# Cross-attention: values become the stationary operand, softmax sums come from products with ones, and the combined heads are made without transposes

## The reference

```python
q = split_heads(x, 16); k = split_heads(ctx, 16); v = split_heads(ctx, 16)   # head size 32
logits = einsum('bhqd,bhkd->bhqk', q, k) + bias                              # 154 keys
weights = softmax(logits * (1.0 / sqrt(32)), axis=-1)
attn = einsum('bhqk,bhkd->bhqd', weights, v)
combined = attn.transpose(0, 2, 1, 3).reshape(B, Sq, 512)
x = layernorm(x + combined @ w_out)
```

## Time and profile before

| | |
|---|---|
| median of 3 runs | 2323.93 us (2323.35 to 2326.02) |
| profiled execution | 2313.03 us, span 2311.2 us |
| mean granted PE clock | 0.954 of full speed |
| PE busy | 2112.9 us, 91% |
| DVE busy | 1764.8 us, 76% |
| ACT busy | 1080.5 us, 47% |
| POOL busy | 839.9 us, 36% |
| cross-attention, first to last value matmul | 586 to 1287 us |

### The profile page before, as it was taken

One profiled execution on the slowest core, in us unless ns is written; L12 is line 12 of the kernel. 1 busy time (PEld: TensorE's weight loads), 2 busy tenths in 40 slices (PEclk: granted clock), 3 DMA queues, 4 the chain that ended last, 5 costly groups with the idle time before them and its releaser, 6 DMA issues. The chain is left out here.

```text
span 2311.2 us, 33151 instructions
## 1 busy us (share of the span) xinstructions
PE 2112.9 (91%) x11904; PEld 1150.9 (50%) x11904; DVE 1764.8 (76%) x3345; ACT 1080.5 (47%) x1522; POOL 839.9 (36%) x819
## 2 busy tenths in 40 slices
PE   7999999984999999999999558899999689999998
PEld 3444444431776776777777323344444234444443
DVE  6768686855787998899998465966666388888885
ACT  1444444442554554555555133344444365555551
POOL 2112221322154555456555532222222134444442
PEclk9999999996798999999999879999999899999999
DMA  6334342457789879869963268888888466666662
GB/s 230 107 137 140 103 154 92 128 124 187 202 186 220 212 175 208 233 166 236 243 164 108 70 216 275 235 267 273 268 273 274 198 211 224 235 223 227 232 224 81
DMA packets 386947, 448.53 MB, mean 194 GB/s; under 512 B 279462, under 2 KB 279750, under 8 KB 368352
## 3 DMA queue, kind: packets, MB, share of 16 engines
q1 hardware_dynamic: 322736, 286.14, 44.0%
q0 software_dynamic: 64048, 160.28, 22.3%
HBM read 259.00 MB, written 138.73 MB: 172 GB/s over the span
## 5 line engine op out<-in xcount | busy, mean ns | idle before, releaser
L1668 PE MATMUL ps_h<-xT,w 128*128 128x512 f16 x2048 | 453.3, 384 | 21.8 <-ACT h L1499 11.9
L1908 PE MATMUL ps<-w,g_hi 128*128 128x512 f16 x1024 | 389.3, 380 | 29.3 <-DVE g_lo L1846 29.3
L1908 PE MATMUL ps<-w,g_lo 128*128 128x512 f16 x1024 | 389.0, 380 | 0.0
L1668 PEld LDWEIGHTS ps_h<-xT,w 128*128 128x128 f16 x2048 | 201.0, 99 | 268.1 <-issue 18.7
L1499 ACT ACTIVATE h<-ps_h,b_in_sb,col_scale 128x512 f32<-128x512 f32 x256 | 197.7, 777 | 261.5 <-PE ps_h L1668 235.1
L1237 PEld LDWEIGHTS ps_o<-vm,pT 128*128 128x128 f32 x2048 | 293.4, 199 | 11.6
L1237 PE MATMUL ps_o<-vm,pT 128*128 128x33 f32 x2048 | 279.6, 262 | 0.0
L1059 DVE TENSOR_REDUCE stack<-ps_m 128x2 f16<-128x308 f32 x512 | 242.8, 476 | 47.7 <-PE ps_m L1191 36.2
L1017 ACT ACTIVATE pT<-logit 128x512 f32<-128x512 f32 x320 | 198.7, 624 | 148.5 <-DVE logit L1077 148.3
L1761 POOL TENSOR_TENSOR rstd<-vare,minus_half 128x1 f32<-128x1 f32 x64 | 154.3, 2411 | 211.9 <-DVE vare L1864 211.9
L1575 DVE TENSOR_REDUCE amax_t<-h 128x1 f32<-128x2048 f32 x64 | 146.2, 2284 | 104.7 <-ACT h L1499 103.7
(11 more groups left out here) (176 smaller groups left out, 3882.1 us busy)
## 6 DMA issues: line engine op xcount, KB each, us to landing
hidden<-h POOLq DMA_DIRECT2D x64, 1024.0 KB, 6.7
hT<-hidden SPq DMA_DIRECT2D x64, 1024.0 KB, 5.9
xc<-x_cols SPq DMA_DIRECT2D x16, 1024.0 KB, 5.2
xr<-x_rows SPq DMA_DIRECT2D x16, 1024.0 KB, 5.5
x_rows<-x POOLq DMA_DIRECT2D x16, 1024.0 KB, 4.8
x1t<-x_rows SPq DMA_DIRECT2D x64, 256.0 KB, 3.6
bt_main<-bias_main SPq DMA_DIRECT2D x16, 1024.0 KB, 6.3
xres<-x_rows SPq DMA_DIRECT2D x64, 256.0 KB, 3.8
```

The source lines that it names most:

```text
L1668: mm = pe.matmul(ps_h[f % 4][:], w1[:, c, f * P:(f + 1) * P], xT[:, e, a, :, c, :], start=(a == 0 and c == 0), stop=(a == 1 and c == KC - 1))
L1908: mm = pe.matmul(ps[t][:], g[:, e, f, t * P:(t + 1) * P], w2[:, f, :], start=(f == 0 and a == 0), stop=(f == FC - 1 and a == 1))
```

## The change

In `values` the operands change places: the values (`vm`, 128 keys x 32, and `vt`, 128 x 128 for the tails of four heads) are stationary, and `pT` moves, 512 tokens at a time. The four heads of a group write four column groups of one `ps_o` (head dimensions on partitions, tokens in the free dimension), onto the product of the tails. `sums` does the same with ones as stationary operand into `ps_s`, which gives the softmax sum of a head on its 32 partitions. `sums` runs at k = 2 and `values` at k = 4, for the group before. DVE takes one reciprocal of 128x512 (`reciprocal_sums`, k = 4) and one multiplication of 128x512 (`normalise`, k = 6) in place of two of each. Since the result is already transposed, ACT and POOL write its two f16 halves into `combT`, and the transposes and their copy are gone. The rest of the diff removes their buffers and semaphores and repacks v_main and v_tail without the column of ones.

```diff
-        vm = sb("vm", [P, 2, HEADS, VW], F32)
-        vt = sb("vt", [P, 2, GROUPS, 4 * VW], F32)
+        vm = sb("vm", [P, 2, HEADS, HD], F32)
+        vt = sb("vt", [P, 2, GROUPS, P], F32)
+        one_main = sb("one_main", [P, HD], F32)
+        one_tail = sb("one_tail", [P, P], F32)
...
+            pool.memset(one_main[:], 1.0).then_inc(ones_ready, 1)
+            pool.memset(one_tail[:], 0.0).then_inc(ones_ready, 1)
+            pool.wait_ge(ones_ready, 2)
+            for j in range(4):
+                pool.memset(one_tail[KTAIL * j:KTAIL * (j + 1), HD * j:HD * (j + 1)], 1.0).then_inc(ones_ready, 1)
+                pool.wait_ge(ones_ready, 3 + j)
...
             def combined_low(s, b, g):
-                if not inside(4 * s + b, g):
-                    return
-                group = 4 * (4 * s + b) + g
-                pool.wait_ge(comb_high, group + 1)
-                if not (isinstance(group, int) and group == 0):
-                    pool.wait_ge(ct_done, group)
-                pool.tensor_tensor(comb_lo[:], comb[:], comb_hi[:], ALU.subtract).then_inc(comb_split, 1)
+                n = 4 * s + b
+                if not inside(n, g):
+                    return
+                pool.wait_ge(comb_high, 4 * n + g + 1)
+                pool.tensor_tensor(combT[:, n % 2, 1, g, :], comb[:], combT[:, n % 2, 0, g, :],
+                                   ALU.subtract).then_inc(comb_split, 1)
...
             def combined_high(nu, g):
                 if not inside(nu, g):
                     return
-                group = 4 * nu + g
-                act.wait_ge(comb_ready, 2 * group + 2)
-                if not (isinstance(group, int) and group == 0):
-                    act.wait_ge(ct_done, group)
-                act.activation(comb_hi[:], comb[:], ACT.Copy).then_inc(comb_high, 1)
-
-            def copy_combined(nu, g, eu):
-                if not inside(nu, g):
-                    return
-                act.wait_ge(ct_done, 4 * nu + g + 1)
-                if not (isinstance(nu, int) and nu < 2):
+                act.wait_ge(comb_ready, 4 * nu + g + 1)
+                if nu >= 2:
                     act.wait_ge(w_done, 4 * (nu - 1))
-                act.activation(combT[:, eu, :, g, :], ps_t16.rearrange("p (a t) -> p a t", a=2),
-                               ACT.Copy).then_inc(ct_ready, 1)
+                act.activation(combT[:, nu % 2, 0, g, :], comb[:], ACT.Copy).then_inc(comb_high, 1)
 
             def quarter(n, i, e):
-                copy_combined(*at(n, i, -3), (e + (i - 3) // 4) % 2)
                 weights(n, i, 0)
+                combined_high(*at(n, i, -2))
                 weights(n, i, 1)
                 weights(n, i, 2)
-                combined_high(*at(n, i, -2))
                 weights(n, i, 3)
                 stack_halves(*at(n, i, 6))
                 weights(n, i, 4)
...
-            def normalise(nu, g, c):
-
+            def reciprocal_sums(nu, g):
                 if not inside(nu, g):
                     return
-                at = 2 * (4 * nu + g) + c
-                o = ps_o[c][:, 0:8 * VW].rearrange("p (a w) -> p a w", w=VW)
-                dve.wait_ge(pv_done, at + 1)
-                if not (isinstance(at, int) and at < 2):
-                    dve.wait_ge(comb_ready, at - 1)
-                dve.reciprocal(rsum[:, c].rearrange("p t h -> p (t h)"), o[:, :, HD]).then_inc(rsum_ready, 1)
-                dve.wait_ge(rsum_ready, at + 1)
-                if not (isinstance(at, int) and at < 2):
-                    dve.wait_ge(comb_split, 4 * nu + g)
-                dve.tensor_tensor(comb[:, c].rearrange("p t (h d) -> p (t h) d", d=HD), o[:, :, 0:HD],
-                                  rsum[:, c].rearrange("p t h -> p (t h)")[:, :, None].to_broadcast([P, 8, HD]),
-                                  ALU.mult).then_inc(comb_ready, 1)
+                group = 4 * nu + g
+                dve.wait_ge(sums_done, group + 1)
+                if group >= 1:
+                    dve.wait_ge(comb_ready, group)
+                dve.reciprocal(rsum[:], ps_s[:]).then_inc(rsum_ready, 1)
+
+            def normalise(nu, g):
+                if not inside(nu, g):
+                    return
+                group = 4 * nu + g
+                dve.wait_ge(pv_done, group + 1)
+                dve.wait_ge(rsum_ready, group + 1)
+                if group >= 1:
+                    dve.wait_ge(comb_split, group)
+                dve.tensor_tensor(comb[:], ps_o[group % 2][:], rsum[:], ALU.mult).then_inc(comb_ready, 1)
...
-                    if k == 1:
-                        normalise(*at(n, i, -2), 1)
                     if k == 7:
                         residual(*at(n, i, -6))
-                    if k == 5:
-                        normalise(*at(n, i, -1), 0)
+                    if k == 4:
+                        reciprocal_sums(*at(n, i, -1))
+                    if k == 6:
+                        normalise(*at(n, i, -1))
...
-            def values(nu, g, eu, t, part):
-
+            def sums(nu, g):
                 if not inside(nu, g):
                     return
-                c = t // 2
-                at = 2 * (4 * nu + g) + c
-                if part == 0 and t % 2 == 0:
-                    pe.wait_ge(exp_done, 5 * (4 * nu + g + 1))
-                    pe.wait_ge(v_in[eu], 32 * (nu // 2 + 1))
-                    if not (isinstance(at, int) and at < 2):
-                        pe.wait_ge(comb_ready, at - 1)
-                base = (t % 2) * 4 * VW
-                tok = slice(t * P, (t + 1) * P)
-                if part == 0:
-                    pe.matmul(ps_o[c][:, base:base + 4 * VW], pT[:, g % 2, 0, tok], vt[:, eu, g, :],
-                              start=(t % 2 == 0), stop=False, skip_group_check=True)
+                group = 4 * nu + g
+                pe.wait_ge(exp_done, 5 * group + 1)
+                if group == 0:
+                    pe.wait_ge(ones_ready, 6)
                 else:
-                    h = part - 1
-                    mm = pe.matmul(ps_o[c][:, base + h * VW:base + (h + 1) * VW], pT[:, g % 2, part, tok],
-                                   vm[:, eu, 4 * g + h, :], start=False, stop=(part == 4 and t % 2 == 1),
-                                   skip_group_check=True)
-                    if part == 4 and t % 2 == 1:
-                        mm.then_inc(pv_done, 1)
-
-            def transpose_combined(nu, g):
+                    pe.wait_ge(rsum_ready, group)
+                pe.matmul(ps_s[:], one_tail[:], pT[:, g % 2, 0, :], start=True, stop=False, skip_group_check=True)
+                pe.wait_ge(exp_done, 5 * (group + 1))
+                for h in range(4):
+                    mm = pe.matmul(ps_s[HD * h:HD * (h + 1), :], one_main[:], pT[:, g % 2, 1 + h, :],
+                                   start=False, stop=True, skip_group_check=True)
+                mm.then_inc(sums_done, 1)
+
+            def values(nu, g, eu):
                 if not inside(nu, g):
                     return
-                pe.wait_ge(comb_split, 4 * nu + g + 1)
-                if not first(4 * nu + g):
-                    pe.wait_ge(ct_ready, 4 * nu + g)
-                for a, half in enumerate((comb_hi, comb_lo)):
-                    for t in range(4):
-                        mm = pe.transpose(ps_t16[:, (4 * a + t) * P:(4 * a + t + 1) * P], half[:, t // 2, t % 2, :],
-                                          ident_h[:])
-                mm.then_inc(ct_done, 1)
+                group = 4 * nu + g
+                pe.wait_ge(v_in[eu], 32 * (nu // 2 + 1))
+                if group >= 2:
+                    pe.wait_ge(comb_ready, group - 1)
+                out = ps_o[group % 2]
+                pe.matmul(out[:], vt[:, eu, g, :], pT[:, g % 2, 0, :], start=True, stop=False, skip_group_check=True)
+                for h in range(4):
+                    mm = pe.matmul(out[HD * h:HD * (h + 1), :], vm[:, eu, 4 * g + h, :], pT[:, g % 2, 1 + h, :],
+                                   start=False, stop=True, skip_group_check=True)
+                mm.then_inc(pv_done, 1)
...
-                    for v in range(20 * k // 8, 20 * (k + 1) // 8):
-                        values(*group, v // 5, v % 5)
-                    if k == 0:
-                        transpose_combined(*at(n, i, -3))
+                    if k == 2:
+                        sums(*at(n, i, -1))
+                    if k == 4:
+                        values(*group)
```

More of the change, by code:

```diff
@@ L36 @@
 GROUPS = HEADS // 4
-VW = HD + 1
 STACK = 3 * HD + 1
@@ L679, in cross_attention_stage @@
         pT = sb("pT", [P, 2, 5, BLK], F32)
[L680 to L683, removed]
+        rsum = sb("rsum", [P, BLK], F32)
+        comb = sb("comb", [P, BLK], F32)
         combT = sb("combT", [P, 2, 2, KC, BLK], F16)
@@ L700, in cross_attention_stage @@
         ps_w = ctx.enter_context(nc.psum_tensor("ps_w", [P, 512], F32))
-        ps_t = ctx.enter_context(nc.psum_tensor("ps_t", [P, 512], F32))
```

(22 more changed lines are left out.)

## The result

The changed kernel takes 2449.15 us (median of 4 runs, 2446.81 to 2452.95) against 2323.64 us before: a ratio of 1.0545, 95% interval 1.0498 to 1.0591. It is slower by about 125 us. The profiled executions are 2452.95 us (span 2451.2) and 2313.03 us (span 2311.2), 140 us apart.

A forecast was written before the change was run, and what follows sets the result against it. PE (88.6 to 89.0 of 90 us) and DVE (80.2 to 85.8) were both taken as nearly full. A quarter (four heads, 512 tokens) would go from 10.9 to 14.7 us, times 64 +245 us: 2570 us, range 2400 to 2690.

The forecast's parts named there:

- signs of being wrong: Blocks under 2 us, DVE not idle behind them, or the clock falling in most quarters would refute the prediction.
- the last step: End of a quarter's chain: k = 2's logit needs the tail bias's buffer, then come the next sums; 0.28 us.
- The column price: On PE: 512 f32 columns take 0.43 us an instruction, two instructions and 0.86 us a product.
- The staggered column groups: In both PE blocks: four column groups overlap only partly, 2.15 us, making a block 3.2 us.
- The reciprocal, 2.4 us, at most 2.9: DVE's 128x512 reciprocal at k = 4: taken as 2.4 us, bounded at 2.9 us, costing nothing beside the values block.
- step 3 of the sum: During PE's 3.2 us values block, DVE does two slices and the reciprocal by 4.8 us; next maxima come at 5.3.
- The sum for DVE alone: DVE's own work in a quarter after the change, put at 11.5 us.
- The chain through a quarter: PE and DVE take turns around the two blocks: 14.7 us a quarter against 10.9, +245 us over 64.
- Rival B: All four column groups at once, block 1.9 us: 2400 us with a fast reciprocal, 2455 with 2.4 us; chance 0.18.
- Rival D: Two buffers carry DVE over the blocks, and DVE with a fast reciprocal sets the quarter: 2285 us; chance 0.06.
- The clock: PE 84% busy might make the granted clock fall: at most +120 us, in the range, none in the forecast.
- Hidden at no cost: ACT's dropped copy, memsets before the stage and smaller v loads: nothing, covered by idle time.

The follow-up runs named there:

- third run: Changed kernel with each f32 product of a column group cut into two of 256 columns, issued in two program orders: 2449.64 us in a single run.
- fifth run: Changed kernel complete, full reciprocal on DVE, with the sums and values blocks cut into four pieces: 2384.40 us, ratio 1.0280 to the kernel before.
- first run: Changed kernel with DVE taking the reciprocal of only 8 of the 512 columns: 2367.59 us, ratio 1.0195 to the kernel before.
- fourth run: Changed kernel with a reciprocal of 8 of the 512 columns and both blocks cut into four pieces of about 1 us: 2309.85 us, ratio 0.9948.
- second run: Kernel before with one unused reciprocal of 128x512 more on DVE in each quarter: 2555.18 us, ratio 1.0989.
- seventh run: Changed kernel complete, with ACT instead of DVE taking the reciprocal as exp(-ln(sum)): 2468.85 us, ratio 1.0643.
- ninth run: Changed kernel, blocks in four pieces, ACT's reciprocal, next tile's q made before it, residual load queued ahead of the transposes: 2305.85 us, ratio 0.9946.

## Why the prediction was right and wrong

The direction held, and so did the range (2400 to 2690); the value of 2570 us was 121 us too high. That the time lies in the range is in part luck. Of the 125 us lost, 81 are the reciprocal, which the forecast put at nothing; with the reciprocal as cheap as assumed, the measured 2368 us lie below the range. And of the forecast's own signs of being wrong one came (blocks under 2 us: 1.95) and another in half (DVE is idle behind the sums block, but not behind the values block); the clock stayed up. The chain as it ran, from the rows after: sums block 1.95, to DVE 0.47, two slices 2.12, the reciprocal to the next maxima 3.27, DVE's work behind it 5.21, the last step 0.28: 13.30 us, where the forecast had 14.7. Point by point:

*The column price, f32 instructions of 0.43 us, two to a product.* Right: the tails' product takes 0.95 us with the change of width behind it.

*The staggered column groups, 2.15 us.* Wrong, and the main error. The step that failed is "I take 2.15, since every row shows matmuls starting in program order": those rows had full-width matmuls, or one instruction to a column group (L1212), and so could not show what two to a group do. The eight instructions take 1.00 us, the block 1.95 and not 3.2 us, and the third run shows that program order doesn't bind the groups. The two blocks were mis-sized by 2.5 us a quarter, 160 us. "TensorEngine Tiling (Array Packing)" in the Trainium skill, section Key Properties, had it right, that tiles operate independently; the trace agrees, with 1.00 us. The in-order starts that the prediction set against it did not hold the groups back.

*The reciprocal, 2.4 us, at most 2.9.* Wrong in size: 3.35 us, 6.2 ns an element more than the first (3348 - 162 over 511). The slope from one to eight elements, 4.6 ns, was not the slope of a long one, and the "upper bound" of 5.3 ns was none. It matters more than was said, for with blocks of 1.95 us its cover is shorter: (step 3 of the sum) the DVE path, 0.47 + 2.12 + 3.27 = 5.9 us, is longer than PE's 1.6 + 1.95 + 0.46 = 4.0 us, and the 3.35 us cost 81 us. The estimate of 4.3 us from "VectorE: DVE Perf Modes" in the Trainium skill was too high by as much as my 2.4 us was too low; the sentence that the small rows contradict it drew too much from them. The sum for DVE alone was wrong too: 10.3 - 1.2 + 0.6 + 2.4 is 12.1 us, not 11.5, and a DVE that sets 12.1 us against the 10.9 of before would by itself have made the kernel slower, as the fifth run's 12.2 us does.

*The chain through a quarter.* Right in kind, and this is what the forecast of "slower" rested on. Rival B's chain with a fast reciprocal was 12.1 us; the first run has 12.09. The match is closer than the reading deserves: B's 6.0 us behind the values block held a running max of 0.78 us where it takes 0.16, and no wait of 0.42 us. PE's 77 to 79 busy us of 90 and DVE's 69 to 70 in that run show both engines with time to spare and the kernel slower than before. Its time, 2368 us, is 32 us under the 2400 us that B gave for this case, half of it since B put the clean 12.1 us against the clean 10.9, while in the mean the quarters are 11.97 us (753.9 / 63) and 11.04.

*Rival B with a slow reciprocal, 2455 us,* came closest (2449). That is luck, for it had two errors that cancel: the reciprocal was 0.95 us longer than in it, and DVE's work behind the values block is 5.2 us instead of 6.0 (1205.44 to 1210.65), among other things because the running max takes 0.16 us and not 0.78.

*Rival D, faster.* Its mechanism needs blocks that DVE can work through. In pieces of about 1 us (fourth run) that happens: 2310 us, but with a reciprocal of eight columns, and still no 2285, for the waits for the residual and the long running max take the rest.

*The clock.* Wrong reasoning, harmless here. PE was busy 80% of the stage and the clock stayed at 1.00 in both stretches shown. In the second run, with PE busy 78 of 90 us (a part of it lengthened by the clock itself), it fell behind standstills of 2.05 us and more; in the seventh it fell too, though PE's longest wait was 1.5 us, as in the changed kernel. So neither the share of busy time that I counted on nor the length of the longest wait tells these kernels apart, and what does stays open.

*Hidden at no cost:* ACT's removed copy, the memsets and the smaller loads were not tested; the chain above closes without them. Most of PE's fall from 89 to 72 busy us of 90 is the longer quarter: a quarter has 10.9 busy us before and 10.6 after. That gain is worth nothing where DVE sets the time.

## What to carry to other kernels

Where two engines go in step through a pair of buffers, the distribution of work over the slices counts as much as its sum: a block longer than what the other engine has in hand costs time, though both are idle for a part of it. Here two blocks of 1.95 us, cut into pieces of 1 us, gave 58 us back. Before a per-token reciprocal is replaced by one that lies replicated across partitions, count its elements along the free dimension: here 16 in a quarter (twice eight) became 512, and DVE, not PE, paid. What a long instruction costs depends on the idle time of the engine that takes it: 75 and 81 us in the two forms of the changed kernel, 231 us in the kernel before, whose DVE was nearly full and whose clock fell.

## What the runs showed of the hardware

- A DVE reciprocal of 128x512 f32 takes 3.35 us, from PSUM and from SBUF (3.34 us in the second run), against 0.68 us for a multiplication of that size.
- f32 matmuls of 32 columns on four column groups run at once: eight instructions of 0.43 us in 1.00 us, sixteen of half the width in 1.00 to 1.02 us, in either program order.
- With PE at a standstill of some 2 us in each quarter the granted clock fell again and again (0.82 in the mean, second run). With a longest standstill of 1.5 us it stayed at 1.00 in the changed kernel and fell to a mean of 0.89 to 0.94 in the seventh run.
- A DVE instruction of one element, the running max, takes from 0.16 to over 1 us. In the list of groups by line (busy us, mean ns of one) of the kernel after, of the fourth run and of the ninth:

```profile
L1132 DVE TENSOR_TENSOR amax_run<-amax_run,amax_t 128x1 f32<-128x1 f32 x64 | 10.2, 159 | 0.3 <-issue 0.3
```
```profile
L1133 DVE TENSOR_TENSOR amax_run<-amax_run,amax_t 128x1 f32<-128x1 f32 x64 | 47.6, 745 | 0.2 <-issue 0.2
```
```profile
L1138 DVE TENSOR_TENSOR amax_run<-amax_run,amax_t 128x1 f32<-128x1 f32 x64 | 59.5, 929 | 0.1
```

  And in the fourth run's timeline, DVE and POOL:

```profile
1206.27 1.16 DVE L1133 TENSOR_TENSOR amax_run<-amax_run,amax_t 128x1 f32<-128x1 f32 x1
...
1206.23 1.17 POOL L931 TENSOR_TENSOR stack<-x1t,q 128x512 f16<-128x512 f32 x1
```

  In the fourth run it ends with a subtraction on POOL that was under way when it began (1206.23 + 1.17 and 1206.27 + 1.16); after the change that subtraction falls elsewhere. That it waits for POOL is what these rows suggest; no run tested it alone. If so, some 50 us of the ninth run could still be had by moving one of the two (59.5 - 64 x 0.16, an estimate).
